# Mixture-of-experts stage of a 32-block loop: second product over 128 array rows in two column halves in place of four 64x64 products

## What is computed

```python
shared = gelu(x @ W1s + b1s) @ W2s + b2s
h = gelu(einsum('bsd,edf->bsef', x, W1p) + b1p)        # 8 experts, 64 -> 256
priv = einsum('bsef,efd->bsed', h, W2p) + b2p          # 256 -> 64
routed = einsum('bsed,bse->bsd', priv, mask)           # mask: two experts of 8 weigh in
return shared + routed
```

## Time and profile before

| | |
|---|---|
| median of 3 runs | 2795.03 us (2794.6 to 2800.79) |
| profiled execution, its own time | 2794.68 us |
| its span in the trace | 2792.3 us |
| mean granted TensorE clock | 0.926 |
| instructions in the span | 191356 |
| expert stage in the trace | from about 2343 us to the end |

### The profile page before, as it was taken

One profiled execution on the slowest core, in us unless ns is written; L12 is line 12 of the kernel. 1 busy time (PEld: TensorE's weight loads), 2 busy tenths in 40 slices (PEclk: granted clock), 3 DMA queues, 4 the chain that ended last, 5 costly groups with the idle time before them and its releaser, 6 DMA issues. The chain is left out here.

```text
span 2792.3 us, 191356 instructions
## 1 busy us (share of the span) xinstructions
PE 2345.5 (84%) x88271; PEld 1460.2 (52%) x88271; DVE 1976.3 (71%) x3247; ACT 1050.1 (38%) x1793; POOL 536.3 (19%) x635
## 2 busy tenths in 40 slices
PE   5799999887999997799999975867477825899998
PEld 3466666644666664466666641223466622444444
DVE  5688888765888885588888860015699964677776
ACT  3433333252333333433333340002044432677776
POOL 1034422101443220034432100000444300000000
PEclk9799999998999998899999986989689958999999
DMA  3266666517999993389999846992222103688886
GB/s 85 68 152 177 168 156 161 148 52 241 325 320 321 313 308 120 120 276 323 324 313 307 269 143 207 427 294 40 84 84 80 54 21 65 124 144 141 142 143 103
DMA packets 242960, 512.67 MB, mean 184 GB/s; under 512 B 65359, under 2 KB 114831, under 8 KB 222159
## 3 DMA queue, kind: packets, MB, share of 16 engines
q1 hardware_dynamic: 233400, 501.71, 62.6%
q10 hardware_dynamic: 9383, 8.55, 1.4%
HBM read 292.25 MB, written 211.63 MB: 180 GB/s over the span
## 5 line engine op out<-in xcount | busy, mean ns | idle before, releaser
L919 ACT ACTIVATE p_v<-p_ps,k_scale_bias 128x1024 f32<-128x1024 f32 x384 | 441.9, 1200 | 882.8 <-PE p_ps L790 882.8
L900 POOL COPY k_xm<-p_sp 64x288 f32<-64x288 f32 x372 | 259.9, 699 | 1175.8 <-DVE p_sp L323 1159.6
L313 DVE STREAM_TRANSPOSE p_vt<-p_v 128x1024 f32<-128x1024 f32 x384 | 451.3, 1214 | 6.1 <-ACT p_v L919 6.1
L790 PEld LDWEIGHTS p_ps<-k_idfty,p_t 32*64 32x64 f32 x24576 | 292.8, 135 | 179.4 <-issue 179.4
L2162 DVE TENSOR_TENSOR x_ht<-x_ht,x_mask 128x384 f32<-128x384 f32 x512 | 262.9, 555 | 144.3 <-ACT x_ht L2133 113.2
L2133 ACT ACTIVATE x_ht<-x_ph,w_b 128x384 f32<-128x384 f32 x576 | 303.4, 578 | 138.0 <-PE x_ph L2185 138.0
L318 DVE STREAM_TRANSPOSE p_at<-p_ps 128x1024 f32<-128x1024 f32 x192 | 228.5, 1229 | 147.7 <-PE p_ps L291 147.7
L790 PE MATMUL p_ps<-k_idfty,p_t 32*64 32x64 f32 x24576 | 320.5, 237 | 11.5 <-issue 11.5
L799 PEld LDWEIGHTS p_ps<-p_vt 128*32 128x32 f32 x24576 | 221.3, 110 | 97.5 <-issue 97.5
L2185 PE MATMUL x_ph<-x_et,w_w 64*64 64x384 f32 x2304 | 245.6, 490 | 10.9 <-DMA x_et<-expert_inputs 6.5
L2201 PE MATMUL x_pe<-x_ht,w_w 64*64 64x384 f32 x2304 | 244.3, 485 | 11.2 <-DVE x_ht L2162 8.5
(11 more groups left out here) (329 smaller groups left out, 2736.4 us busy)
## 6 DMA issues: line engine op xcount, KB each, us to landing
field<-p_v SPq DMA_DIRECT2D x768, 256.0 KB, 5.6
p_v<-field SPq DMA_DIRECT2D x128, 1024.0 KB
x_mask<-expert_weights SPq DMA_DIRECT2D x32, 1536.0 KB, 14.3
l_v<-field SPq DMA_DIRECT2D x16, 2048.0 KB, 26.8
k_xm<-field SPq DMA_DIRECT2D x12, 2048.0 KB, 28.7
at_cf<-state_coefficients SPq DMA_DIRECT2D x32, 384.0 KB
k_mixw<-field SPq DMA_DIRECT2D x4, 2048.0 KB, 27.2
k_mixw<-in_L_tok_fw_dram SPq DMA_DIRECT2D x48, 144.0 KB, 4.2
```

The costliest lines, as they stand in the source:

```text
L313: return nc.vector.transpose(cols(vt), cols(px.rearrange("p (g m) -> p g m", g=G)))
L790: ins = nc.tensor.matmul(ps[64 * a1:64 * a1 + 64, g, col:col + S], lines, K["idfty"][rows, :], start=False, stop=True, skip_group_check=True)
L900: nc.gpsimd.tensor_copy(view[64 * k:64 * k + 64, :, j, :, G * i:G * i + G], sp[64 * j:64 * j + 64, :, :, 16 * k:16 * k + M1].rearrange("p ...
L919: nc.scalar.activation(field[:, 2 * q:2 * q + 2, CH * half:CH * half + CH], ps[:, e, 2 * q:2 * q + 2, :], ACT.Relu, bias=bias, scale=scale ...
```

## The change

The second product of a step takes all 128 rows of a tile at once, in one column half of the array for each tile, and writes bank 0 alone. `totals` is one copy, which now signals `s_ready`. Bank 1 still receives half of what `turn` writes. Nothing else differs.

```diff
@@ totals(i, par), VectorE @@
                 dve.wait_ge(s.fx_done, (E + 1) * (i + 1))
                 at_least(dve, s.um_done, i)
-                ve.tensor_copy(total[:, :], ps_e[:, par, 0, 0:CT]).then_inc(s.tt_done, 1)
-                dve.wait_ge(s.tt_done, i + 1)
-                ve.tensor_tensor(total[:, :], total[:, :], ps_e[:, par, 1, 0:CT], ALU.add).then_inc(s.s_ready, 1)
+                ve.tensor_copy(total[:, :], ps_e[:, par, 0, 0:CT]).then_inc(s.s_ready, 1)
@@ outputs(i, par, e), TensorE @@
                 for half in range(2):
-                    for c in range(2):
-                        rows = slice(D * c, D * c + D)
-                        ins = nc.tensor.matmul(ps_e[D * half:D * half + D, par, c, 0:CT], w2[rows, e, half, :],
-                                               ht[rows, (2 * e + half) % 6, :], start=(e == 0), stop=(e == E),
-                                               skip_group_check=True)
+                    ins = nc.tensor.matmul(ps_e[D * half:D * half + D, par, 0, 0:CT], w2[:, e, half, :],
+                                           ht[:, (2 * e + half) % 6, :], start=(e == 0), stop=(e == E),
+                                           skip_group_check=True)
                 ins.then_inc(s.fx_done, 1)
```

## The result

The changed kernel takes 2848.84 us (median of 4 runs, 2842.46 to 2855.09) where the kernel before takes 2796.63 (median of 4, 2794.6 to 2800.79). The ratio is 1.0182, 95% interval 1.0147 to 1.0218: slower by 1.8%, as forecast in direction. The forecast was 2861.5 us, in a range of 2843 to 2886: +67 us were forecast and +52 were measured.

The account below looks back on a forecast made before the run. TensorE's sequence was taken to bound the kernel. Profiled 2794.7 + 83.9 (seams) - 16.5 (totals) - 0.5 (first mask wait) = 2861.6 us, predicted as 2861.5 us, range 2843 to 2886 us.

Parts of the forecast that it names:

- What bounds the kernel: Expert stage: TensorE, busy 96%, sets the pace; changes to its sequence count in full, VectorE's only through one wait.
- The stream: nothing: Second-product groups of 128 rows x 64 columns stay at 0.645 us inside, weight loads hidden; no change.
- The seams, 0.16 and 0.15 us, 540 of them: Form changes between first and second products: 286 at 0.16 us, 254 at 0.15 us, +83.9 us.
- The totals, 16.5 us: VectorE's second totals instruction goes: 0.53 us back at the turn in 30 blocks, 0.58 us in the last.
- the three seams of cover: Between VectorE's tile 6 and the turn: 0.47 us of extra cover, so 15.9 us return even with the addition kept.
- Other edits, "half as many O instructions: nothing": Halving second-product instructions changes nothing, as the 0.32 us stream decides; VectorE otherwise nothing; first mask wait in block 0, -0.5 us.
- one thing of weight: In 380 us TensorE's only sizeable wait: the turn, for the totals' second instruction, 12.9 us in 28 pieces.
- no seam: Rival, 5%: at borders of first and second products nothing drains, only the gain stays, 2778 us.
- halves one after the other: Rival, 2%: column halves run in sequence, each second-product group takes 1.29 us, 186 us more, 3048 us.
- loads not hidden: Rival, 3%: each second-product group's second pass also has an open 0.05 us load, 14 us more, 2876 us.
- wait kept: Rival, 2%: something other than the addition holds the turn, so the 15.9 us stay, 2878 us.
- clock: Rival, 3%: pauses at every border lower the granted clock below 1.00; 5% of the streams, 19 us, 2880 us.

Follow-up runs that it names:

- one-form kernel: The changed kernel with the first product also in 128 rows x 64 columns from block 1 on, half of that product left out: 2778.14 us, ratio 0.9933.
- pairs kernel: The changed kernel with steps taken in pairs, two groups of first products then two of second, rows behind tile 12: 2811.87 us, ratio 1.0070.
- The two kernels that tried for the gain alone: The kernel before with the turn one step later, rows behind tile 12: 2800.08 us; with the totals' copy moved from behind tile 6 to tile 4: 2791.06 us.

## Why the prediction was right or wrong

**What bounds the kernel**: right. TensorE's sequence counted in full; in the changed kernel it waits for nobody from 2400 to 2830 us.

**The stream: nothing**: right. The one-form kernel runs the 128*64 product at 0.645 us a group.

**The seams, 0.16 and 0.15 us, 540 of them**: right in mechanism and size. A pair of groups takes 1.60 us where it took 1.29, 0.31 for the two borders, and the pairs kernel gives 0.15 for each border removed. The steady block was put at 15.25 us and is 15.24.

**The totals, 16.5 us**: right as a term of the sum against the kernel before, since the 0.53 us at each turn are gone. It wasn't the edit's own merit, though: with the instruction put back only 3 us are lost, as the prediction's aside on the three seams of cover had it, but for 0.08 us a block. The two kernels that tried for the gain alone in the kernel before, forecast at 2781 us, missed: moved, the wait turned into a wait for masks; split, it met the mask loads.

**Other edits, "half as many O instructions: nothing"**: this is the step that missed, together with the list of waits that I read as holding "one thing of weight". The earlier trace rows has a second one, 3.2 us in one piece before L2185 with "issue" as its releaser, and I put the profile's whole time into the sum as if it were all rhythm. In the stage the sum was 83.9 - 16.5 - 0.5 = +66.9 us; the stage grew by 57.0 us (442.9 to 499.9 from its first pass to its last). The pauses that went are 8.9 of the 9.9 us between; they are absent from every kernel with fewer passes a block, even at blocks of 12.58 us, so the term set at nothing was worth about 9 us here. The rest of the miss lies outside: the two profiles reach the stage at 2345.7 and 2342.4 us, 3.3 us apart with nothing changed in between.

**The rivals**: no seam, halves one after the other, loads not hidden, wait kept, and clock are all refuted by the timeline, the waits and the windows above. On the third the Trainium skill ("TensorE: Matmul & The Clock Gate", The mechanism) says that weight loads overlap running matmuls only where the row group differs. In the changed kernel all passes of a second product use all rows, and its group lasts 0.87 us with one load open, no longer than the 0.88 us of the 64*64 group, where the row groups do differ. In the one-form kernel, where all rows are used by both products, groups of 0.645 us leave no load open: a weight load starts 2 ns behind the start of a pass over the same rows (2604.187 and 2604.185 us). As far as the sentence on row groups goes, the measurement decides against it; the same section also lets a load go ahead of running matmuls into a background weight buffer, and with that the trace agrees.

**The range** held the time only near its lower end. Its bounds came from the price of a seam, which was known best; the term that missed had no bounds at all.

## What to carry to other kernels

Count the changes of array form in TensorE's order, as one counts instructions: on a bound engine each costs a drained array and an open weight load, 0.15 us for 64 columns here, which is a quarter of a 0.645 us group. Group products of one form, or keep the neighbour's form, before making one product "larger". In the profile such a loss hides in a busy share of 100%; start-to-start times show it. And before summing against a profiled time, divide it into its steady rhythm times the number of rounds and a remainder, and ask of the remainder whether the change keeps it.

## What the runs showed of the hardware

TensorE stopped for up to 4.6 us at a time while code was run for the first time, at the same passes in the kernels with two blocks written out ahead of the loop: 9 us in the kernel before and 23 us with eight more blocks written out. The same written-out length costs nothing in the changed kernel, whose blocks stay at 15.24 us. Writing out a loop isn't free where TensorE takes 26 instructions per microsecond; at 20 and fewer it nearly was.

A removed wait uncovered the next resource twice: the masks' computation when the turn was moved (13.22 us a block), then the masks' loads when the totals were split (12.59 to 13.6 us). Only with loads in halves did the 12.59 us hold in every steady block.
